# An LSTM step with two gates packed in each 32 PSUM rows by a stationary of zero columns and h

## What is computed

```python
xz = einsum('ntd,dk->ntk', x, Wx) + b
def step(carry, xz_t):
    prev_h, prev_c = carry
    ai, af, ao, ag = split(xz_t + prev_h @ Wh, 4, axis=1)
    next_c = sigmoid(af) * prev_c + sigmoid(ai) * tanh(ag)
    next_h = sigmoid(ao) * tanh(next_c)
    return (next_h, next_c), next_h
x = x + scan(step, (cond, 0), xz)
x = x + adapter(x, cond)      # two products with 256 x 256 matrices, a gelu, rank-8 parts
```

## Time and profile before

| | us |
|---|---|
| median of 3 runs | 621.93 (621.92 to 622.44) |
| span of the profiled execution, first to last instruction | 618.6 |
| PE busy | 600.8 (97%) |
| PEld (weight loads) busy | 444.2 (72%) |
| DVE busy | 471.6 (76%) |
| ACT busy | 386.8 (63%) |

### The profile page before, as it was taken

How to read it: one execution, slowest core, us unless ns; L and a number is a source line. 1 busy time by engine, 2 the same in 40 slices (tenths; PEclk the granted TensorE clock), 3 DMA queues, 4 the chain that set the end, 5 groups by cost and what they waited for, 6 DMA issues and landing times.

```text
span 618.6 us, 33951 instructions
## 1 busy us (share of the span) xinstructions
PE 600.8 (97%) x14120; PEld 444.2 (72%) x14120; DVE 471.6 (76%) x2543; ACT 386.8 (63%) x2158; POOL 38.6 (6%) x77
## 2 busy tenths in 40 slices
PE   8689998999999999999999999999999999999997
PEld 5565556777777777777777777777777777777886
DVE  3576667778888888788888888888878888888772
ACT  2365656666666666666666666666666666666662
POOL 3000000000000000000000000000000000000000
PEclk9899999999999999999999999999999999999999
DMA  5993630232333123333321232332122323211201
GB/s 162 233 217 141 181 45 13 38 46 55 55 55 53 32 33 49 54 55 54 56 34 32 47 54 55 54 55 41 38 33 55 55 55 55 44 37 24 54 21 36
DMA packets 31499, 38.74 MB, mean 63 GB/s; under 512 B 3632, under 2 KB 29536, under 8 KB 30321
## 3 DMA queue, kind: packets, MB, share of 16 engines
q1 hardware_dynamic: 31282, 36.51, 30.5%
q0 software_dynamic: 64, 0.07, 0.1%
HBM read 15.59 MB, written 4.19 MB: 32 GB/s over the span
## 4 chain that ended last, share of the span: by engine, by line
PE 95%; DVE 1%; issue 1%; DMA 1%; SPq 0%; ACT 0%; ACTq 0%
PE z L698 36%; PE x_bank L496 18%; PE z_o L698 9%; PE aux L522 8%; PE out_bank L545 7%; PE out_bank L627 3%; PE aux L507 3%; PE aux L474 2%; PE out_bank L577 2%; PE aux L529 2%; PE out_bank L566 1%; PE x_bank L566 1%; DMA seed<-proj 1%; PE x_bank L522 1%; DMA x_nat<-in_x 0%
## 5 line engine op out<-in xcount | busy, mean ns | idle before, releaser
L698 PEld LDWEIGHTS z<-wh,h_t 128*16 128x16 f32 x8160 | 159.8, 96 | 116.8 <-DVE h_t L855 87.1
L698 PE MATMUL z<-wh,h_t 128*16 128x96 f32 x8160 | 233.5, 248 | 4.9 <-issue 2.1
L835 DVE STREAM_TRANSPOSE z<-z 128x96 f32<-128x96 f32 x512 | 151.4, 298 | 86.7 <-PE z L698 67.9
L413 ACT ACTIVATE gates<-z 128x48 f32<-128x48 f32 x512 | 107.7, 210 | 156.9 <-DVE z L835 129.3
L496 PE MATMUL x_bank<-wx,x_t 128*128 128x256 f32 x512 | 156.0, 392 | 0.5 <-ACT x_t L331 0.5
L337 ACT ACTIVATE z<-seed 128x96 f32<-128x96 f32 x512 | 123.7, 242 | 5.8 <-DMA seed<-proj 5.8
L698 PE MATMUL z_o<-wh,h_t 128*16 128x64 f32 x4080 | 106.1, 219 | 0.8 <-issue 0.8
L845 DVE SCALAR_TENSOR_TENSOR prod<-gates 128x32 f32<-128x32 f32 x512 | 97.7, 191 | 0.6
L850 DVE SCALAR_TENSOR_TENSOR gates<-prod 128x16 f32<-128x16 f32 x512 | 84.2, 165 | 8.7
L496 PEld LDWEIGHTS x_bank<-wx,x_t 128*128 128x128 f32 x512 | 80.6, 195 | 6.4 <-issue 1.5
L698 PEld LDWEIGHTS z_o<-wh,h_t 128*16 128x16 f32 x4080 | 81.2, 97 | 1.4 <-issue 1.3
(11 more groups left out here) (114 smaller groups left out, 439.0 us busy)
## 6 DMA issues: line engine op xcount, KB each, us to landing
seed<-proj SPq DMA_DIRECT2D x128, 128.0 KB
w<-in_L_cond_W SPq DMA_DIRECT2D x4, 2048.0 KB, 10.2
x_nat<-in_x SPq DMA_DIRECT2D x32, 128.0 KB, 4.2
out<-y_nat SPq DMA_DIRECT2D x32, 128.0 KB, 4.2
wx<-in_L_cond_Wx SPq DMA_DIRECT2D x2, 512.0 KB, 5.9
wh<-in_L_cond_Wh SPq DMA_DIRECT2D x2, 256.0 KB, 7.1
wh<-in_L_cond_Wh SPq DMA_DIRECT2D x1, 512.0 KB, 6.5
w<-in_L_cond_W SPq DMA_DIRECT2D x1, 256.0 KB, 4.5
```

What stands on the lines that cost most here:

```text
L413: act.activation(gates[s % 2][m][:, 0:3 * B].rearrange("p (g b) -> p g b", b=B), zt[m].rearrange("p (g c) -> p g c", c=C)[:, :, 0:B], ACT. ...
L698: ins = pe.matmul(dst, h_prev[:, kc, :], rhs, start=False, stop=(kc == 1), skip_group_check=True)
L835: dve.transpose(zt[m], z_bank[m][:, 0:GC]).then_inc(turned[m], 1)
```

## The change

z of a step is laid out more tightly. Each 32 rows of PSUM hold two gates: rows 0 to 15 one, rows 16 to 31 another. A matmul cannot start its output at row 16 of a column group, so the lower gate is computed with a stationary of 32 columns, 16 of zeros and 16 of h (`h_t` and `h_first` now hold zeros in front of h), which adds nothing to rows 0 to 15 and h @ Wh to rows 16 to 31. A half then takes 64 columns and gate o 32. The transposes are 64 and 32 columns wide, and ScalarE reads and writes contiguous columns. The three gates of a half come from two matmuls per kc and j, one of 32 and one of 64 moving columns; gate o from two of 32. A step has 48 matmuls where it had 24.

The order on TensorE stays half 0 kc 0, wait for `ht_ready[1]`, half 0 kc 1, half 1, gate o. The seeds come by eight DMAs a block, each half as wide. On ScalarE the seed copies are moved: seed 0 right behind gates 0, seed 1 right behind gates 1; and the wait for a block's seeds is moved from the end of step 6 to the head of step 7.

```diff
-GC = 3 * C
-OC = NM * C
-ZW = NM * GC + OC
+ZC = NM * C
+OC = C
+Z_AT = (0, ZC + OC)
+O_AT = ZC
+SW = 2 * ZC + OC
+HW = SW - C
@@ load_seed
                 for j in range(NQ):
-                    sp.dma_start(seed[f.par][32 * j:32 * j + B, :, :], proj[f.par][:, ZW * j:ZW * (j + 1)])\
+                    low, high = 2 * HW * j, 2 * HW * j + HW
+                    sp.dma_start(seed[f.par][32 * j + B:32 * j + 2 * B, :, 0:HW], proj[f.par][:, low:high])\
+                      .then_inc(seed_loaded[f.par], 16)
+                    sp.dma_start(seed[f.par][32 * j:32 * j + B, :, C:SW], proj[f.par][:, high:high + HW])\
                       .then_inc(seed_loaded[f.par], 16)
@@ ScalarE, one_block
+                    if s == TB - 1 and more:
+                        act.wait_ge(seed_loaded[ahead.par], (ahead.turn + 1) * (32 * NQ))
                     gates_of(0)
+                    if more:
+                        seed_bank(ahead.par, s_next, 0)
                     gates_of(1)
+                    if more:
+                        seed_bank(ahead.par, s_next, 1)
                     tanh_o()
                     tanh_cell(0)
-                    if more:
-                        act.wait_ge(gates_ready[0], n)
-                        seed_bank(ahead.par, s_next, 0)
                     tanh_cell(1)
                     if more:
-                        act.wait_ge(gates_ready[1], n)
-                        seed_bank(ahead.par, s_next, 1)
                         act.wait_ge(ht_ready[1], n + 1)
                         seed_o(ahead.par, s_next)
@@ TensorE, one_block
+                    def recur(kc, dst, cols, low, done=None):
+
+                        for j in range(NQ):
+                            rows = slice(32 * j, 32 * j + (2 * B if low else B))
+                            ins = pe.matmul(dst(rows), h_prev[:, kc, 0:2 * B] if low else h_prev[:, kc, B:2 * B], cols(j),
+                                            start=False, stop=(kc == 1), skip_group_check=True)
+                        if done:
+                            ins.then_inc(done, 1)
...
+                    def half_0(kc, done=None):
+                        recur(kc, z_cols(0, C, 1), units_of(kc, 0, 1, 0), False)
+                        recur(kc, z_cols(0, 0, 2), units_of(kc, 1, 2, 0), True, done)
+
+                    def half_1(kc, done=None):
+                        recur(kc, z_cols(1, 0, 1), units_of(kc, 2, 1, 1), True)
+                        recur(kc, z_cols(1, 0, 2), units_of(kc, 0, 2, 1), False, done)
+
+                    def gate_o_cols(kc, done=None):
+                        recur(kc, o_cols, units_of(kc, 3, 1, 1), False)
+                        recur(kc, o_cols, units_of(kc, 3, 1, 0), True, done)
+
+                    pe.wait_ge(ht_ready[0], n)
+                    pe.wait_ge(seeded[0], n)
+                    half_0(0)
+                    pe.wait_ge(ht_ready[1], n)
+                    half_0(1, z_ready[0])
+                    pe.wait_ge(seeded[1], n)
+                    half_1(0)
+                    half_1(1, z_ready[1])
+                    pe.wait_ge(seeded_o, n)
+                    gate_o_cols(0)
+                    gate_o_cols(1, zo_ready)
@@ VectorE
+            dve.memset(h_first[:, :, 0:B], 0.0).then_inc(h_padded, 1)
+            for i in range(2):
+                dve.memset(h_t[i][:, :, :, 0:B], 0.0).then_inc(h_padded, 1)
@@ turn
-                dve.transpose(zt[m], z_bank[m][:, 0:GC]).then_inc(turned[m], 1)
+                dve.transpose(zt[m], z_bank[m][:, 0:ZC]).then_inc(turned[m], 1)
```

More of the change, by code:

```diff
@@ L106, in lstm_adapter @@
         proj = [sb(f"proj{i}", [P, G * H]) for i in range(2)]
-        seed = [sb(f"seed{i}", [P, TB, ZW]) for i in range(2)]
-        h_first = sb("h_first", [P, NM, B])
+        seed = [sb(f"seed{i}", [P, TB, SW]) for i in range(2)]
+        h_first = sb("h_first", [P, NM, 2 * B])
         gates = [[sb(f"gates{i}_{m}", [P, 4 * B]) for m in range(NM)] for i in range(2)]
@@ L113, in lstm_adapter @@
         prod = [sb(f"prod{m}", [P, 2 * B]) for m in range(NM)]
-        h_t = [sb(f"h_t{i}", [P, NM, TB, 32]) for i in range(2)]
+        h_t = [sb(f"h_t{i}", [P, NM, TB, 2 * B]) for i in range(2)]
         xp = [sb(f"xp{i}", [P, NM, P]) for i in range(2)]
@@ L131, in lstm_adapter @@
         tanc = [tanc_bank[:, 0:B], o_bank[:, 2 * OC:2 * OC + B]]
-        zt = [z_bank[m][:, GC:2 * GC] for m in range(NM)]
+        zt = [z_bank[m][:, ZC:2 * ZC] for m in range(NM)]
         zt_o = o_bank[:, OC:2 * OC]
+        at_gates = (B, 0)
         mid_bank, up_bank = (aux, x_bank[0]), (out_bank, x_bank[1])
@@ L181, in gate_cols @@
         def gate_cols(t, gate):
[L183 to L187, removed]
+            first, step = PLACES[gate]
+            eighths = t[:, :].rearrange("p (j e c) -> p e j c", j=NQ, c=C)
+            return eighths[:, first:first + step + 1:step]
         class Blk:
@@ L335, in seed_bank @@
             def seed_bank(buf, s, m):
-                act.activation(z_bank[m][:, 0:GC], seed[buf][:, s, GC * m:GC * (m + 1)], ACT.Copy)\
+                act.activation(z_bank[m][:, 0:ZC], seed[buf][:, s, Z_AT[m]:Z_AT[m] + ZC], ACT.Copy)\
                    .then_inc(seeded[m], 1)
             def seed_o(buf, s):
-                act.activation(o_bank[:, 0:OC], seed[buf][:, s, NM * GC:ZW], ACT.Copy).then_inc(seeded_o, 1)
+                act.activation(o_bank[:, 0:OC], seed[buf][:, s, O_AT:O_AT + OC], ACT.Copy).then_inc(seeded_o, 1)
             def gelu_mid(a):
@@ L645, in _ @@
             for i in range(WARM_UP):
-                ins = pe.matmul((*z_bank, o_bank)[i % 3][:, 0:GC], zeros[:, :], zeros[:, 0:GC], start=True, stop=True)
+                ins = pe.matmul((*z_bank, o_bank)[i % 3][:, 0:ZC], zeros[:, :], zeros[:, 0:ZC], start=True, stop=True)
             ins.then_inc(bits_set, 1)
@@ L673, in one_block @@
                     if s > 0:
-                        h_prev = h_t[k.par][:, :, s - 1, 0:B]
+                        h_prev = h_t[k.par][:, :, s - 1, :]
                     elif k.at_least(1):
-                        h_prev = h_t[1 - k.par][:, :, TB - 1, 0:B]
+                        h_prev = h_t[1 - k.par][:, :, TB - 1, :]
                     else:
[L678 to L687, removed]
-                        gates_of = wh[:, kc, :].rearrange("p (g u) -> p g u", g=G)
[L689 to L701, removed]
@@ new lines, in units_of, with z_cols, o_cols @@
+                    def units_of(kc, first, n, m):
+                        gates_of = wh[:, kc, :].rearrange("p (g u) -> p g u", g=G)
+                        return lambda j: gates_of[:, first:first + n, m * P + C * j:m * P + C * (j + 1)]
+                    def z_cols(m, lo, n):
+                        return lambda rows: z_bank[m][rows, lo:lo + n * C].rearrange("p (g c) -> p g c", c=C)
+                    def o_cols(rows):
+                        return o_bank[rows, 0:OC].rearrange("p (g c) -> p g c", c=C)
@@ L844, in cell_products @@
                 dve.wait_ge(gates_ready[m], n)
-                dve.scalar_tensor_tensor(prod[m][:, :], now[:, 0:2 * B], 1.0, now[:, 2 * B:4 * B],
+                i_f, g_c = ((now[:, B:3 * B], now[:, :].rearrange("p (q b) -> p q b", b=B)[:, 0:4:3]) if m == 0 else
+                            (now[:, 0:2 * B], now[:, 2 * B:4 * B].rearrange("p (q b) -> p q b", b=B)))
+                dve.scalar_tensor_tensor(prod[m][:, :].rearrange("p (q b) -> p q b", b=B),
+                                         i_f.rearrange("p (q b) -> p q b", b=B), 1.0, g_c,
                                          ALU.add, ALU.mult).then_inc(prod_ready[m], 1)
@@ L937, in add_h @@
                                        x_t[k.k % N_X][:, m, :].rearrange(tokens, b=B),
-                                       h_t[k.par][:, m, :, 0:B].rearrange("p t b -> p b t"), ALU.add)\
+                                       h_t[k.par][:, m, :, B:2 * B].rearrange("p t b -> p b t"), ALU.add)\
                         .then_inc(xp_ready, 1)
```

32 lines of the change are left out of this document (15 added, 17 removed).

## The result

The changed kernel took 840.36 us in the median of 6 runs (835.70 to 842.00), the kernel before, run in turn with it, 622.18 (6 runs). The ratio is 1.3505, 95% interval 1.3472 to 1.3538: slower by 35%. The profiled execution took 836.5 with a span of 834.7, at a mean granted clock of 0.986.

What follows compares the result with a forecast made beforehand. A loop through all engines bounds the kernel before, TensorE's instruction refill the changed one. 22.8 us to the first block's end, 2.6 start, 828 for 208 blocks, about 5 at the end: span 858, median 861, stated 860; range 720 to 970.

Steps and rivals of the forecast that it cites:

- The bound: TensorE's instruction refill limits every block: 208 blocks of 256 instead of 112, used up in 2.7 us, shortest seen 3.4.
- The size: Time per TensorE instruction block: delay 1.53, packet 1.15, landing to use 1.3, together 3.98 us; 208 blocks are 828 us.
- the delay: From TensorE's entry into a block to the next packet's start: 1.15 us entered early, 2.3 late, 1.53 taken.
- landing to use: From an instruction packet's landing to TensorE going on with that block: 1.3 us.
- the 858 of the sum: Forecast span in us: 22.8 until the first block is used up, 2.6, 828, about 5 for last jobs and stores.
- ScalarE's order "at nothing": Seed copies moved in front of gates 1 and tanh o cost nothing, covered by ScalarE's idle 37%; uncovered, up to 0.24 us.
- The start: First seeds by eight DMAs instead of four, on the chain that starts the recurrence: 2.6 us more.
- Transposes: Narrower transposes, 298 to 257 ns and the o one about 41 less: 0.03 to 0.04 us a step, nothing when starved.
- The rival of the clock: Starved PE's clock falls to its 1.2 GHz level and passes take twice as long: above 1000 us; chance 0.04.
- The refill does not get ahead (616): Denied rival: next request goes out while the last packet is in flight, shorter transposes decide, 616 us; chance 0.08.
- the time does not stay as it was (620 to 623): Denied rival: refill keeps up, transposes' gain eaten by doubled pass starts and start-up, 620 to 623 us; chance 0.02.
- Short passes do get shorter: Denied rival: 32-column passes take as long as 64-column ones, 110 us in all, about 730 without starvation; chance 0.03.

Runs made afterwards that it cites:

- experiment 1: The changed kernel with one matmul in place of two per kc, bank and column group, leaving out part of the computation: 612.00 us, ratio 0.9859.
- experiment 2: The kernel before with 24, 8 or 4 added zero matmuls a step (the 4 are 96 columns wide): 925.91, 711.12 and 673.62 us.
- experiment 3: The changed kernel with ScalarE's order and seed wait of the kernel before: 912.07 us.
- wide24: The kernel of experiment 1: the changed layout with 24 matmuls a step instead of 48, 612.00 us, ratio 0.9859 to the kernel before.
- before_act: The kernel before with ScalarE's new order of seed copies and seed wait alone: 617.99 us, ratio 0.9940.
- after_swap: The changed kernel with TensorE's two waits at a step's head exchanged, so the one for h 0 stands alone: 899.73 us.
- experiments 3 to 5: In this order the runs of after_oldact, pad24_act and after_swap: 912.07, 864.23 and 899.73 us.
- after_oldact: The kernel of experiment 3: the changed kernel with ScalarE's old order and seed wait, 912.07 us.
- pad24: The kernel before with 24 more zero matmuls of 16 columns a step, 96 instructions, in front of the last o group: 925.91 us.
- pad24_act: The kernel before with 24 zero matmuls of 16 columns a step and ScalarE's new order: 864.23 us.
- ctl4: The kernel before with 4 more zero matmuls a step, 96 columns wide, 16 instructions: 673.62 us.
- pad8: The kernel before with 8 more zero matmuls of 16 columns a step, 32 instructions: 711.12 us.

## Why the prediction was right, point by point

*The bound.* The prediction said that an unseen resource, the refill of TensorE's instructions, would become the limit of every block. 208 packets came, 96% of the blocks are starved, experiment 1 takes the loss away with the second half of the matmuls, and experiment 2 brings it into the old layout with matmuls that compute nothing. The next block is fetched during the current one, but only one, at 3.9 us each, and at 206 instructions for a step of 2.2 us it is hardly ever hidden. The Trainium skill, "Runtime: NRT & Kernel Launch" (Instruction fetch mechanics), has it mostly hidden; the trace of the changed kernel disagrees, with 96% of the blocks starved.

*The size.* The forecast was 3.98 us a block, the measurement 3.89. The term that was mis-sized is the delay: "two thirds at 1.15 and one third at 2.3, 1.53". It was 1.33. Against that landing to use was 1.37, not 1.3, and the 4% of blocks that were not starved add the rest: 1.33 + 1.14 + 1.37 + 0.05 = 3.89. 208 x 0.09 is 19 us, most of the 23 by which the span, 834.7, fell below the 858 of the sum; the other 4 or 5 lie in what was added for the start and the end. The two values 1.15 and 2.3 are the two cases of the kernels in which the stand-alone wait passes late; what I had not seen is what decides between them. I put it down to the place in the run of z and guessed a third. It is a wait, and the change itself moved the moment at which that wait passes: in the changed kernel only 4% of the starved blocks have a delay of 2 us or more, with ScalarE's old order 40%. That 1.53 came so near 1.33 is in part luck.

*ScalarE's order "at nothing".* Wrong. The copies cost nothing where I looked, on ScalarE. But seed 0 ends earlier, TensorE's stand-alone wait passes earlier, and the refill goes out earlier: 72 us (experiment 3). With the old order my one third at 2.3 would have been too small: 1.70 was measured and 912 us.

*The start.* Forecast 2.6 us later for four more seed DMAs. The chain of waits of the changed kernel (start, us, what):

```profile
18.47 0.60 SPq L257
19.11 2.34 DMA seed<-proj
...
21.91 1.48 PE z L687 x64
```

The last DMA is issued 3.2 us later than in the earlier trace rows, but it lands after 2.34 us where the last of four took 4.69, and the first z passes start at 21.91 instead of 21.13: 0.8 us, not 2.6.

*Transposes.* 265 and 228 ns for the 257 and 216 forecast. That narrower ones are worth about 8 us when nothing starves was close: `wide24` gives 0.9859 and `before_act` 0.9940, so the layout is worth 0.8%, 5 us, of which the transposes alone were not measured.

*The rival of the clock.* It did not happen as stated: the mean granted clock stayed near full. But the low level does occur. In the changed kernel the clock is low in a few stretches; in `after_swap`, with longer cuts, in more. Windows of `after_swap`, columns as in the earlier trace rows:

```profile
372.40:376.00 3.60, 3.34 (x66) 2.62 (x69) 0.88 (x6) 0.96 (x5) 0.00 (x0) 0.53 0.02 5
376.00:380.00 4.00, 3.98 (x169) 3.21 (x156) 3.21 (x18) 2.22 (x15) 1.01 (x2) 1.00 0.08 20
```

0.53 is nearly all at 1.2 GHz, and 66 passes were made in 3.6 us. The mean is 0.960 here and 0.986 in the changed kernel, so some 72 and 23 us were spent at the low level (twice the missing share, times the span). A slow stretch is not free in a starved kernel. In `after_swap` 19 blocks have 1 us or more at the low level; they took 5.09 us each, and those wholly at the high level 4.08, which makes 19 us in all; in the changed kernel it is 6 us. Longer cuts stand ahead of these stretches, so not all of that is the clock's price. It leaves experiments 3 to 5 as they are: of the blocks wholly at the high level the mean is 3.85 us in the changed kernel, 4.17 in `after_oldact` and 4.08 in `after_swap`, 4.19 in `pad24` and 3.90 in `pad24_act`. Over 207 blocks these differences are 66, 48 and 60 us, of 76, 63 and 62 between the profiled executions.

*The other rivals.* The refill does not get ahead (616), and the time does not stay as it was (620 to 623). Short passes do get shorter (197 ns in the mean for 32 columns, 219 for 64).

## What to carry to other kernels

Count TensorE's instructions per microsecond beside its columns. In this unrolled program a block of 256 instructions needs 3.4 to 4.2 us, and up to 5 where the stand-alone wait passes late. So some 110 in a step of 2.2 us were already near the edge (16% starved), and the narrower layout was worth 5 us, where the matmuls that it took made the whole 218 us slower. Where a stream is near that edge, the wait that stands alone at the head of a loop should be one that passes early: which of two waits that is, and when the engine that feeds it gets to it, was worth 59 to 72 us in these starved kernels.

## What the runs showed that I had not expected

- A request for the next block of instructions waits behind a stand-alone semaphore wait that is some 15 to 75 instructions ahead: delay 2.3 us instead of 1.15. Two lines exchanged in the text cost 7% (`after_swap`, 899.7 us for 840.4).
- One block is in use and one is coming, in the twelve kernels run here: of some 2,000 blocks, about 10 show their next packet start before TensorE entered the block that landed last, by 0.55 us at most, which can be records missing from the count of 256. No packet starts less than 2.27 us behind the landing of the one before. The Trainium skill, "Advanced Engine Details and Errata" (ISA Cache), gives a line of 16 KB, 256 instructions, and only two lines; the 208 packets of 3.41 MB agree.
- 16 more instructions a step, 14% more packets, took the share of starved blocks from 16 to 47% (`ctl4`), and 32 more cost 90 us (`pad8`). The edge is steep: the kernel before was on it, and only "issue" in a few places showed it.
- Twice as many passes with half the columns in the mean took no longer, as the PE timeline of one step of the changed kernel shows (columns as in the earlier trace rows):

```profile
348.07 0.88 PE L687 MATMUL z<-wh,h_t 128*16 128x32 f32 x64
348.77 0.48 PE L687 MATMUL z_o<-wh,h_t 128*16 128x32 f32 x32
```

64 passes, half of them of 32 and half of 64 columns, end 0.88 us after the first began, where 32 of 96 columns took 0.91. Less the last pass of 0.2 us, that is 0.68 / 63 = 11 ns from start to start. Within one of the four column groups it is four times that, some 44 ns, so neither this row nor that of the o passes in the prediction shows that one column group starts passes closer than 25 ns.
- The clock fell to 1.2 GHz for single stretches behind cuts of 1.5 to 3.5 us, but not behind most of the cuts of the changed kernel, which are 1.0 to 1.6 us long: between 100 and 180 us of it the granted clock was 1.00.
